# Mean rows of the context products in one operand of 36 partitions, and a last product that finishes its last two tiles one by one

## The chip, the cores and the metric

The kernel runs on one core of a Trainium2 chip, in one launch. The metric is the device time of an execution in microseconds. The core's engines run their own instruction streams and meet only at semaphores: PE (TensorE, matrix products into PSUM), DVE (VectorE), ACT (ScalarE), POOL (GpSimd) and SP, which here only issues transfers.

## The reference, cut to what matters

Three stages are added onto x (2 x 512 tokens, width 1024), in float32; each begins with a layer norm without weights:

```python
x = x + attn_block(layernorm(x))                 # Mamba2 block and a gated MLP of 3584
x = x + matmul(fake_quant(layernorm(x)), fake_quant(ctx))   # per batch [512,1024] x [1024,1024]
x = x + ffn(layernorm(x))                        # gate, up and down of 3584
# layernorm:  (x - mean) / sqrt(var + 1e-5)
# fake_quant: q = clip(round(x / s + zp), 0, 255);  (q - zp) * s
# ffn weights: W = base + mean(|w - base|) * sign(w - base)
```

Both inner widths are 3584, so that each of the two MLPs (m = 0 and m = 1 below) is three products of 1024 tokens with 1024 x 3584 weights.

## The kernel before, in words

**Layout.** x lies on the chip as x transposed: 128 channels on the partitions, 8 such tiles (`KT`) for 1024 tokens (`TOK`); a half of it is one batch of 512 tokens (`H`). One matmul has 128 x 128 weights and 512 columns. Products in float32 accuracy are made of three matmuls in a rounded format (hi x hi, lo x hi, hi x lo); ACT or DVE makes the hi parts, DVE the lo parts. The MLPs are computed by Winograd products of blocks: gate and up at L1067 (L1011 for a few plain ones ahead), down at L1092, as two blocks (`sc`) of 7 products (`t`) in each MLP, so that d = 14 m + 7 sc + t runs over 28 down products, and d = 27 is the last one of the program. A down product has 7 steps (k, `SC_PAIRS`), one per pair of weight tiles in a ring of 7 slots, and 4 output tiles (q) in 4 PSUM banks: 7 x 4 x 3 = 84 matmuls. `down_step` issues them step by step, with q inside k, so all four tiles end together; semaphore `s_pd` then tells DVE, which adds or subtracts the 4 tiles into x (`down_out`, L1914, one instruction of 128 x 512 each). In the last product of all, each such sum is followed by a store of the tile by SP (L739).

**Order.** PE executes in the order in which the code issues. First x's statistics (L848), then the Mamba2 block, MLP m = 0, the context stage, MLP m = 1. PE is not alone in setting the pace: in the context stage DVE and ACT normalise and round x while PE multiplies the rounded part of it. All weights of MLP m = 1 are made up by DVE, ACT and POOL ahead of PE, in the order of the steps (`ring_hi`, `ring_lo`, `comb_hi`, `comb_lo`).

**Context stage.** For each batch b, `ctx_first` (L1133 to L1144) walks the 8 input tiles k as ACT delivers them (`s_q1`) and makes 4 output tiles at once (L1125, integers in bf16); after each k a small matmul (L1139) multiplies row sums of the other operand, `g_parts`, 4 columns wide (three bf16 parts of the sum, and a column of ones), into rows 0 to 3 of a PSUM bank. ACT (`rows_hi`, L1643) and DVE (`rows_lo`, L2314) turn these rows, scaled by -1/1024, into a hi and a lo part of 4 rows each, two tiles of `xm_r`. `minus_mean` (L1130) then subtracts the mean over the output channels from an output tile with two matmuls of 3 rows, hi and lo, weights all one. The other 4 output tiles follow (`second_tile`). DVE takes each tile into x (`ctx_take`, L2327) and squares it; PE sums the squares for the variance (`ctx_var`, L1119, L1122). `second_mean` (L1148) makes the mean of the next layer norm from the 4 rows, hi and lo, as float32 matmuls, which are two instructions each. DVE takes that at L2320, then works out the next layer norm's scale and starts on the inputs of MLP m = 1, PE begins the products of m = 1 at L1011.

**Constants.** At the start DVE fills constants (L1690 ff.), scales for the quantisation (L1709 to L1716), and only then squares x (L2033), for which PE waits at L848.

## Time and profile before

| | |
|---|---|
| median of 3 runs | 2143.09 us (2141.26, 2143.09, 2144.04) |
| the profiled execution's own time | 2142.7 us |
| its span | 2140.9 us |
| mean granted TensorE clock over it | 0.993 of full |
| PE busy | 2101.9 us (98%), 9270 matmuls |
| DVE busy | 1664.3 us (78%) |
| ACT, POOL busy | 1071.0 us (50%), 182.5 us (9%) |
| PE in the chain that ended last | 87%; DVE 7%, ACT 3%, issue 2%, DMA 1% |

The span goes from the first to the last instruction that the profiler recorded, the execution's own time is 1.8 us longer. Busy time is time in which an instruction was in execution; that of PE counts matmuls, whose weight loads (PEld) overlap other matmuls. The chain that ended last follows the last instruction back to what it waited for, step by step; only a change to a piece in this chain can shorten the time at once, and then only until another chain takes its place.

### The profile page before, as it was taken

The numbers are of one execution on the slowest core, as the hardware profiler recorded it, in microseconds if no ns is written. First come the engines' busy times: TensorE is split into PE (matmuls) and PEld (weight loads), VectorE is DVE, ScalarE is ACT, GpSimd is POOL, SyncE is SP. The second block draws the span as 40 slices with busy tenths as digits, with TensorE's granted clock in tenths as the row PEclk, the third lists the DMA queues.
The fourth block names the chain that finished last, engine by engine and source line by source line (L and its number), as shares of the span: only waits on it lengthen the run. The fifth ranks groups of instructions, "written<-read, shape, count | busy, mean of one in ns | idle before, by whom it ended". The sixth has DMA issues, their size and how long they took to land.

```text
span 2140.9 us, 26618 instructions
## 1 busy us (share of the span) xinstructions
PE 2101.9 (98%) x9270; PEld 1680.6 (78%) x9270; DVE 1664.3 (78%) x2497; ACT 1071.0 (50%) x1764; POOL 182.5 (9%) x296
## 2 busy tenths in 40 slices
PE   7999999999999999999999999999999999999999
PEld 3777778777888888888888854888888888888887
DVE  7766666698777888887979888987777677698885
ACT  4333344466777777775444466543333333444442
POOL 0000110101111111210000001100010000100000
PEclk9999999999999999999999999999999999999999
DMA  3141115638989999889250043654444443856101
GB/s 123 40 169 66 59 60 171 160 78 293 316 285 316 344 323 340 307 313 341 83 193 1 1 151 101 174 197 151 177 151 145 175 148 135 301 186 202 56 20 59
DMA packets 136435, 370.06 MB, mean 173 GB/s; under 512 B 16689, under 2 KB 27569, under 8 KB 132657
## 3 DMA queue, kind: packets, MB, share of 16 engines
q1 hardware_dynamic: 111216, 288.16, 39.3%
q0 software_dynamic: 25088, 80.23, 11.0%
q8 instruction: 73, 1.20, 0.2%
q14 instruction: 58, 0.47, 0.1%
HBM read 288.12 MB, written 84.41 MB: 174 GB/s over the span
## 4 chain that ended last, share of the span: by engine, by line
PE 87%; DVE 7%; ACT 3%; issue 2%; DMA 1%; SPq 0%; DVEq 0%; ACTq 0%
PE pair L1067 42%; PE pair L1092 24%; PE pair L839 7%; PE pair L1011 4%; PE pair L832 2%; DVE conv_out L2098 1%; PE pair L1125 1%; PE pair L949 1%; PE pair L970 1%; DVE pair L1922 1%; DVE weights_lo L1688 1%; PE pair L848 1%; PE pair L1119 1%; PE pair L972 1%; PE pair L865 0%
## 5 line engine op out<-in xcount | busy, mean ns | idle before, releaser
L1067 PE MATMUL pair<-comb_hi,ring_hi 128*128 128x512 f32 x1456 | 567.0, 389 | 3.3 <-ACT gate_a L1400 3.3
L1067 PE MATMUL pair<-comb_hi,ring_lo 128*128 128x512 f32 x1456 | 566.5, 389 | 0.0
L1067 PE MATMUL pair<-comb_lo,ring_hi 128*128 128x512 f32 x1456 | 566.4, 389 | 0.0
L1092 PE MATMUL pair<-inner_ring_a,ring_hi 128*128 128x512 f32 x1120 | 344.9, 389 | 0.0
L1067 PEld LDWEIGHTS pair<-comb_hi,ring_hi 128*128 128x128 f32 x1456 | 273.3, 188 | 62.5 <-DVE ring_lo L1778 5.3
L1067 PEld LDWEIGHTS pair<-comb_lo,ring_hi 128*128 128x128 f32 x1456 | 273.4, 188 | 56.7
L1067 PEld LDWEIGHTS pair<-comb_hi,ring_lo 128*128 128x128 f32 x1456 | 273.3, 188 | 56.5
L1092 PEld LDWEIGHTS pair<-inner_ring_a,ring_hi 128*128 128x128 f32 x1120 | 210.2, 188 | 43.5
L1092 PE MATMUL pair<-inner_ring_a,ring_lo 128*128 128x512 f32 x560 | 217.9, 389 | 0.0
L1322 ACT ACTIVATE ring_hi<-ring_sum 128x512 fp32r<-128x512 f32 x160 | 101.4, 633 | 143.7 <-DVE ring_sum L1763 142.0
L1778 DVE TENSOR_TENSOR ring_lo<-raw_a,ring_hi 128x512 fp32r<-128x512 f32 x146 | 99.9, 689 | 52.6 <-ACT ring_hi L1322 52.6
L1092 PE MATMUL pair<-inner_ring_b,ring_hi 128*128 128x512 f32 x448 | 138.3, 390 | 0.0
L1448 ACT ACTIVATE sign_out<-pair 128x1024 int8<-128x1024 f32 x84 | 86.1, 1025 | 80.7 <-DVE pair L1922 80.7
L1092 PEld LDWEIGHTS pair<-inner_ring_a,ring_lo 128*128 128x128 f32 x560 | 105.1, 188 | 21.9
L1778 DVE TENSOR_TENSOR ring_lo<-ring_sum,ring_hi 128x512 fp32r<-128x512 f32 x160 | 110.0, 687 | 2.2 <-ACT ring_hi L1322 0.9
L839 PE MATMUL pair<-act_hi,weights_hi 128*128 128x512 f32 x256 | 109.4, 427 | 1.7 <-DVE act_lo L2167 1.4
L1922 DVE TENSOR_TENSOR pair<-coeff_in 128x1024 f32<-128x1024 f32 x84 | 103.2, 1228 | 0.0
L1688 DVE TENSOR_TENSOR weights_lo<-weights_raw,weights_hi 128x1024 fp32r<-128x1024 f32 x44 | 54.6, 1241 | 59.4 <-ACT weights_hi L1245 31.0
L839 PE MATMUL pair<-act_hi,weights_lo 128*128 128x512 f32 x256 | 100.3, 392 | 0.0
L839 PE MATMUL pair<-act_lo,weights_hi 128*128 128x512 f32 x256 | 100.1, 391 | 0.0
L1092 PEld LDWEIGHTS pair<-inner_ring_b,ring_hi 128*128 128x128 f32 x448 | 84.1, 188 | 17.8 <-issue 0.5
L1322 ACT ACTIVATE ring_hi<-raw_a 128x512 fp32r<-128x512 f32 x146 | 90.4, 626 | 10.7 <-DVE raw_a L1758 7.1
(374 smaller groups left out, 3591.8 us busy)
## 6 DMA issues: line engine op xcount, KB each, us to landing
coeff_in<-f_gu SPq DMA_DIRECT2D x56, 512.0 KB, 5.2
coeff_in<-b_gu SPq DMA_DIRECT2D x56, 512.0 KB, 6.8
weights_raw<-w_mamba SPq DMA_DIRECT2D x44, 512.0 KB, 3.5
raw_a<-w_gu SPq DMA_DIRECT2D x28, 512.0 KB, 7.1
raw_a<-w_gu SPq DMA_DIRECT2D x56, 256.0 KB, 6.3
u_spill<-gate_a POOLq DMA_DIRECT2D x56, 256.0 KB, 5.8
coeff_in<-f_dn SPq DMA_DIRECT2D x28, 512.0 KB, 4.3
coeff_in<-b_dn SPq DMA_DIRECT2D x28, 512.0 KB, 6.1
```

The source lines that it names most:

```text
L832: ins = pe.matmul(out[:, HALF[half]], w[:, wi, k * P:(k + 1) * P], a(half, k), start=k == 0 and n == 0, stop=k == KT - 1 and n == 2)
L839: ins = pe.matmul(out, w[:, wi, k * P:(k + 1) * P], a(b, k), start=k == 0 and n == 0, stop=k == KT - 1 and n == 2, skip_group_check=True)
L848: return pe.matmul(out[:, HALF[b]], ones[:, :], src[:, HALF[b]], start=first, stop=last)
L949: pe.matmul(ps[2][:, g * 512:(g + 1) * 512], bx_cur[:, 2 + g, :], xbc[:, 4 + g * HPG:4 + (g + 1) * HPG, b * SEQ + c * P:b * SEQ + (c + 1) ...
L1011: ins = pe.matmul(out, wt[:, slot, col], a, start=j % 2 == 0 and kk == 0 and n == 0, stop=j % 2 == 1 and kk == KH - 1 and n == 2, skip_gro ...
L1067: ins = pe.matmul(out, wt[:, slot, col], a, start=t in (0, 1, 3) and kk == 0 and n == 0, stop=kk == KH - 1 and n == 2, skip_group_check=True)
L1092: ins = pe.matmul(out, wt[:, slot, col], a, start=t in (0, 1, 3) and k == 0 and n == 0, stop=k == SC_PAIRS - 1 and n == 2, skip_group_chec ...
L1322: act.activation(WRH[:, slot, :], src, ACT.Copy).then_inc(s_whi, 1)
L1448: act.activation(sign_out[:, c % 2, :], dif_ps[:, :], ACT.Sign).then_inc(s_sign, 1)
L1688: TT(WL[:, slot, :], raw[:, rslot, :], WH[:, slot, :].bitcast(F32), ALU.subtract).then_inc(s_ready, 1)
L1778: TT(WRL[:, slot, :], src, WRH[:, slot, :].bitcast(F32), ALU.subtract).then_inc(s_wlo, 1)
L1922: TT(dif_ps[:, :], dif[:, c % 2, 0, :], dif[:, c % 2, 1, :], ALU.subtract).then_inc(s_cd, 1)
```

## The change

Two parts, and some small ones that they need.

**One operand for the mean rows.** `g_parts` is 36 columns wide: 0 to 2 and 32 to 34 hold the three parts, 3 and 35 are one, the others zero. The small matmul of `ctx_first` gives rows 0 to 35; `rows_hi` writes the rounded rows 0 to 35, `rows_lo` writes the rest over rows 32 to 35 of the same tile. So `minus_mean` and `second_mean` are one matmul of 36 rows in place of two of 3 or 4 rows. Their weights need a zero or a factor per row, which DVE works out at the start (four more small operations, a fifth one that was in `ctx_left_factors`, and two small memsets); `ctx_left_factors` becomes two instructions, `q2_parts` gets one more copy. The buffer `ones_rounded` moves, since `g_parts` grew, and is filled later, in `decay_rows`. The semaphore `s_dtc` is merged into `s_dts`.

**The last product.** `down_step` for d = 27 issues tiles q = 0 and 1 step by step (6 matmuls per step), then all 7 steps of q = 2 (21 matmuls), then all 7 of q = 3. `s_last` is raised after q = 1 and after q = 2, `s_pd` after q = 3, and `down_out` waits for them in turn.

The diff, cut:

```diff
@@ -274,11 +275,15 @@
-    def mean_rows(b, part):
-        return xm_r[0:4, 2 * part + b, 0:H]
-    ones_rows = xm_r[0:3, 4, 0:P]
-    row_weights = xm[0:4, 5, 0:P]
+    ROWS = slice(0, 36)
+    LOW_ROWS = slice(32, 36)
+    def mean_rows(b, rows):
+        return xm_r[rows, b, 0:H]
+    ones_rows = xm_r[ROWS, 4, 0:P]
+    row_weights = xm[ROWS, 5, 0:P]
...
@@ -372,11 +377,10 @@
     g_rest = small("q2_row_sums_rest", [P, CTX_TILES])
-    g_parts = small("q2_row_sums_bf16", [P, CTX_TILES, 4], BF16)
+    g_parts = small("q2_row_sums_bf16", [P, CTX_TILES, 36], BF16)
     mean_col = small("mean_columns", [P, 3, BATCH])
-    row_scale = small("row_scale", [P, 2])
+    row_scale = small("row_scale", [P, 4])
     pick = small("minus_head_pick", [P, HEADS])
-    ones_r = small("ones_rounded", [P, P], F32R)
     tri, ident, mask = shp[:, 0, :], shp[:, 1, :], shp[:, 2, :]
...
@@ -1068,6 +1072,21 @@
+        def last_tiles(w, m, k, qs):
+            slot, us = w % RING, (w - BASE_D[m]) % RING
+            for q in qs:
+                out = bank(4 + q)
+                col = slice(q * P, (q + 1) * P)
+                for n, (wt, a) in enumerate(((WRH, ur_hi(us)), (WRH, ur_lo(us)), (WRL, ur_hi(us)))):
+                    ins = pe.matmul(out, wt[:, slot, col], a, start=False,
+                                    stop=k == SC_PAIRS - 1 and n == 2, skip_group_check=True)
+                if k == SC_PAIRS - 1 and q == 1:
+                    ins.then_inc(s_last, 1)
+                elif k == SC_PAIRS - 1 and q == 2:
+                    ins.then_inc(s_last, 1)
+            if qs == (3,):
+                ins.then_inc(s_pd, 1)
         def down_step(w, m, sc, t, k):
...
@@ -1084,6 +1103,14 @@
                         pe.wait_ge(s_ab, CF_BLOCKS)
+            if m == 1 and d == 13:
+                last_tiles(w, m, k, (0, 1))
+                if k == SC_PAIRS - 1:
+                    for q in (2, 3):
+                        for kk in range(SC_PAIRS):
+                            last_tiles(w - k + kk, m, kk, (q,))
+                return
             slot, us = w % RING, u % RING
...
@@ -1126,9 +1153,7 @@
         def minus_mean(b, out):
-            for part in range(2):
-                ins = pe.matmul(out, ones_rows, mean_rows(b, part)[0:3], start=False, stop=part == 1, skip_group_check=True)
-            ins.then_inc(s_xo, 1)
+            pe.matmul(out, ones_rows, mean_rows(b, ROWS), start=False, stop=True, skip_group_check=True).then_inc(s_xo, 1)
...
@@ -1136,7 +1161,7 @@
                     ctx_mm(b, o, k, banks[o])
-                ins = pe.matmul(rows[0:4, :], g_parts[:, b * KT + k, :], q1[b][:, k, :], start=k == 0, stop=k == KT - 1)
+                ins = pe.matmul(rows[ROWS, :], g_parts[:, b * KT + k, :], q1[b][:, k, :], start=k == 0, stop=k == KT - 1)
                 if k == late:
...
@@ -1144,9 +1169,7 @@
         def second_mean(b, out):
-            for part in range(2):
-                ins = pe.matmul(out, row_weights, mean_rows(b, part).bitcast(F32), start=part == 0, stop=part == 1)
-            ins.then_inc(s_csumd, 1)
+            pe.matmul(out, row_weights, mean_rows(b, ROWS).bitcast(F32), start=True, stop=True).then_inc(s_csumd, 1)
...
@@ -1640,7 +1663,7 @@
             act.wait_ge(s_row, b + 1)
-            act.activation(mean_rows(b, 0), bank(5)[0:4, :], ACT.Copy, scale=-1.0 / DM).then_inc(s_rhi, 1)
+            act.activation(mean_rows(b, ROWS), bank(5)[ROWS, :], ACT.Copy, scale=-1.0 / DM).then_inc(s_rhi, 1)
...
@@ -1699,7 +1722,6 @@
         dve.memset(coef3[:, :], 0.0)
-        dve.tensor_copy(ones_r[:, :], ones[:, :])
         own.then(TT(pick[:, :], ident[:, 0:HEADS], ident[:, PART_AT[1]:PART_AT[1] + HEADS], ALU.add))
...
@@ -1714,6 +1736,14 @@
         own.then(TS(row_scale[:, 0:1], D2, -float(DM), 1.0, ALU.mult, ALU.add))
+        for first in (0, 32):
+            dve.memset(g_parts[:, :, first + 3:first + 4], 1.0)
+        own.then(TT(row_scale[:, 3:4], ident[:, 3:4], ident[:, 35:36], ALU.add))
+        own.then(TS(row_scale[:, 1:2], row_scale[:, 3:4], row_scale[:, 0:1], -1.0, ALU.mult, ALU.add))
+        own.then(dve.tensor_reduce(row_scale[:, 2:3], ident[:, 0:3], mybir.AxisListType.X, ALU.add))
+        own.then(dve.tensor_reduce(row_scale[:, 3:4], ident[:, 32:35], mybir.AxisListType.X, ALU.add))
+        own.then(TT(row_scale[:, 2:3], row_scale[:, 2:3], row_scale[:, 3:4], ALU.add))
...
@@ -1908,8 +1938,15 @@
                     dve.wait_ge(s_do, 4 * d)
-                dve.wait_ge(s_pd, w + 1)
+                if d < 27:
+                    dve.wait_ge(s_pd, w + 1)
                 for q in range(KH):
+                    if d == 27 and q == 0:
+                        dve.wait_ge(s_last, 1)
+                    elif d == 27 and q == 2:
+                        dve.wait_ge(s_last, 2)
+                    elif d == 27 and q == 3:
+                        dve.wait_ge(s_pd, w + 1)
                     tile = X[m][:, QROW[quad] + q, COL[m][QCOL[quad]]]
...
@@ -2000,11 +2037,13 @@
             hi, mid, lo = (g_parts[:, :, n] for n in range(3))
+            low_rows = g_parts[:, :, 32:35]
             own.then(dve.tensor_copy(hi, g_all[:, :]))
             own.then(TT(g_rest[:, :], g_all[:, :], hi, ALU.subtract))
             own.then(dve.tensor_copy(mid, g_rest[:, :]))
             own.then(TT(g_rest[:, :], g_rest[:, :], mid, ALU.subtract))
-            dve.tensor_copy(lo, g_rest[:, :]).then_inc(s_cp, 1)
+            own.then(dve.tensor_copy(lo, g_rest[:, :]))
+            dve.tensor_copy(low_rows, g_parts[:, :, 0:3]).then_inc(s_cp, 1)
...
@@ -2077,6 +2116,7 @@
             top = slice(0, PARTS_K)
+            dve.tensor_copy(ones_r[:, :], ones[:, :])
             own.then(dve.tensor_copy(cs_rows[top, :], ps[3][top, :]))
...
@@ -2276,9 +2316,8 @@
         def ctx_left_factors():
-            dve.tensor_copy(ones_rows, ones[0:3, :])
-            own.then(TS(row_scale[0:4, 1:2], shp[0:4, 1, 3:4], row_scale[0:4, 0:1], -1.0, ALU.mult, ALU.add))
-            TS(row_weights, ones[0:4, :], row_scale[0:4, 1:2], None, ALU.mult).then_inc(s_mc, 1)
+            TS(ones_rows, ones[ROWS, :], row_scale[ROWS, 2:3], None, ALU.mult)
+            TS(row_weights, ones[ROWS, :], row_scale[ROWS, 1:2], None, ALU.mult).then_inc(s_mc, 1)
...
@@ -2311,7 +2350,8 @@
             dve.wait_ge(s_rhi, b + 1)
-            STT(mean_rows(b, 1), bank(5)[0:4, :], -1.0 / DM, mean_rows(b, 0).bitcast(F32), ALU.mult, ALU.subtract).then_inc(s_rlo, 1)
+            STT(mean_rows(b, LOW_ROWS), bank(5)[LOW_ROWS, :], -1.0 / DM, mean_rows(b, LOW_ROWS).bitcast(F32),
+                ALU.mult, ALU.subtract).then_inc(s_rlo, 1)
...
```

On PE, at the end of the context stage, after the last tile of `second_tile` (`x_mid_rounded` is the tile with the mean rows). Before:

```order
L1130 MATMUL pair<-x_mid_rounded 128x512 x4
L1125 MATMUL pair<-q_1_162,q_163 128x512 x16
L1130 MATMUL pair<-x_mid_rounded 128x512 x4
L1119 MATMUL pair<-x_mid,ones_over_dm 128x512 x3
L1122 MATMUL pair<-x_mid,ones_over_dm 128x512 x2
L1148 MATMUL pair<-x_mid_rounded,x_mid 128x512 x4
L1011 MATMUL pair<-comb_hi_82,ring_hi 128x512
```

Now:

```order
L1156 MATMUL pair<-x_mid_rounded 128x512 x2
L1152 MATMUL pair<-q_1_163,q_164 128x512 x16
L1156 MATMUL pair<-x_mid_rounded 128x512 x2
L1146 MATMUL pair<-x_mid,ones_over_dm 128x512 x3
L1149 MATMUL pair<-x_mid,ones_over_dm 128x512 x2
L1172 MATMUL pair<-x_mid_rounded,x_mid 128x512 x2
L1015 MATMUL pair<-comb_hi_83,ring_hi 128x512
```

Every group of mean matmuls has half as many; what stands between them is in the same order. L1156 was L1130, L1172 was L1148, both with 36 rows now.

On PE, in the last product (`pair2` holds the banks of q = 0 and 1, `pair3` those of q = 2 and 3; x2 is two matmuls). Before, the last eight rows of the program:

```order
L1092 MATMUL pair2<-inner_ring_b_136,ring_hi_131 128x512 x2
L1092 MATMUL pair2<-inner_ring_b_136,ring_lo_132 128x512
L1092 MATMUL pair2<-inner_ring_b_136,ring_hi_131 128x512 x2
L1092 MATMUL pair2<-inner_ring_b_136,ring_lo_132 128x512
L1092 MATMUL pair3<-inner_ring_b_136,ring_hi_131 128x512 x2
L1092 MATMUL pair3<-inner_ring_b_136,ring_lo_132 128x512
L1092 MATMUL pair3<-inner_ring_b_136,ring_hi_131 128x512 x2
L1092 MATMUL pair3<-inner_ring_b_136,ring_lo_132 128x512
```

Now:

```order
L1081 MATMUL pair2<-inner_ring_b_137,ring_hi_132 128x512 x2
L1081 MATMUL pair2<-inner_ring_b_137,ring_lo_133 128x512
L1081 MATMUL pair2<-inner_ring_b_137,ring_hi_132 128x512 x2
L1081 MATMUL pair2<-inner_ring_b_137,ring_lo_133 128x512
L1081 MATMUL pair3<-inner_ring_a_135,ring_hi_132 128x512 x2
L1081 MATMUL pair3<-inner_ring_a_135,ring_lo_133 128x512
L1081 MATMUL pair3<-inner_ring_a_135,ring_hi_132 128x512 x2
L1081 MATMUL pair3<-inner_ring_a_135,ring_lo_133 128x512
```

Before, each step goes over both halves, and the four tiles end within 12 matmuls of each other. Now `pair2` ends first; behind it stand 42 matmuls, 21 on q = 2 and then 21 on q = 3, which begin again with the first inner tile (`inner_ring_a`).

On DVE, from the last constants to the first squares of x. Before:

```order
L1713 TENSOR_SCALAR quant_columns<-quant_columns 128x1
L1714 TENSOR_TENSOR quant_columns<-quant_columns 128x1
L1715 TENSOR_TENSOR quant_columns<-quant_columns 128x1
L1716 TENSOR_SCALAR row_scale<-quant_columns 128x1
L2033 TENSOR_TENSOR conv_out<-hs 128x512 x4
```

Now:

```order
L1736 TENSOR_TENSOR quant_columns<-quant_columns 128x1
L1737 TENSOR_TENSOR quant_columns<-quant_columns 128x1
L1738 TENSOR_SCALAR row_scale<-quant_columns 128x1
L1740 MEMSET q_row_sums_bf_190 128x16 x2
L1742 TENSOR_TENSOR row_scale<-tri_ident_mask 128x1
L1743 TENSOR_SCALAR row_scale<-row_scale 128x1
L1744 TENSOR_REDUCE row_scale<-tri_ident_mask 128x1
L1745 TENSOR_REDUCE row_scale<-tri_ident_mask 128x1
L1746 TENSOR_TENSOR row_scale<-row_scale 128x1
L2072 TENSOR_TENSOR conv_out<-hs 128x512 x4
```

Seven small instructions stand between L1738 (was L1716) and the squares L2072 (was L2033); five of them wait for one another through `own.then`. The cast of `ones_rounded`, 128 x 128, has gone from ahead of these rows.

## Rows read from the trace of the kernel before

**Rows 1.** The page: its first line and section 1.

```profile
span 2140.9 us, 26618 instructions
...
PE 2101.9 (98%) x9270; PEld 1680.6 (78%) x9270; DVE 1664.3 (78%) x2497; ACT 1071.0 (50%) x1764; POOL 182.5 (9%) x296
```

**Rows 2.** The chain that ended last, whole span: start us, us, what.

```profile
7.89 5.73 PE pair L848 x8
...
1373.74 495.27 PE pair L1067 x2184
```

**Rows 3.** The same chain, asked for from 1276 to 1332 us.

```profile
1297.20 0.31 PE pair L1139
1297.51 0.97 PE pair L1125 x4
...
1304.97 1.12 PE pair L1130 x4
...
1315.56 0.67 PE pair L1130 x2
...
1318.48 4.51 PE pair L1119 x6
...
1324.70 3.62 PE pair L1148 x8
```

**Rows 4.** Timeline of DVE: start us, us, engine line operation, [idle before <-releaser].

```profile
6.41 0.16 DVE L1715 TENSOR_TENSOR quant_columns<-quant_columns 128x1 f32<-128x1 f32 x1
6.60 0.15 DVE L1716 TENSOR_SCALAR row_scale<-quant_columns 128x1 f32<-128x1 f32 x1
7.05 0.69 DVE L2033 TENSOR_TENSOR conv_out<-hs 128x512 f32<-128x512 f32 x1 [0.29 <-DMA hs<-x_t]
8.76 0.69 DVE L2033 TENSOR_TENSOR conv_out<-hs 128x512 f32<-128x512 f32 x1 [1.02 <-DMA hs<-x_t]
```

**Rows 5.** Groups by form: line engine operation, shapes xcount | busy us, mean ns | idle before.

```profile
L917 PEld LDWEIGHTS pair<-tri_ident_mask,minus_cs_wide 128*72 128x72 f32 x16 | 1.8, 143 | 0.1
...
L1139 PEld LDWEIGHTS pair<-q,q_row_sums_bf 128*4 128x4 bf16 x16 | 1.3, 80 | 6.8 <-issue 6.8
```

**Rows 6.** The same view for PE.

```profile
L942 PE MATMUL pair<-cs_rhs,ones_rounded 72*128 72x512 f32 x16 | 5.2, 404 | 2.9 <-DVE conv_out L2098 2.9
```

**Rows 7.** Timeline of DVE around the context stage.

```profile
1280.30 0.69 DVE L2292 SCALAR_TENSOR_TENSOR scratch_c<-scratch_c 128x512 f32<-128x512 f32 x1 [1.47 <-ACT scratch_c L1619]
...
1316.33 1.41 DVE L2327 SCALAR_TENSOR_TENSOR centred<-pair,quant_columns,centred 128x512 f32<-128x512 f32 x2 [2.08 <-PE pair L1130]
...
1328.44 0.75 DVE L2320 SCALAR_TENSOR_TENSOR scratch_c<-pair,quant_columns,scratch_c 128x512 f32<-128x512 f32 x1 [0.97 <-PE pair L1148]
...
1369.93 0.70 DVE L1778 TENSOR_TENSOR ring_lo<-raw_even,ring_hi 128x512 fp32r<-128x512 f32 x1
```

**Rows 8.** Timeline of PE at the wait for ACT, and at product step 15.

```profile
1296.16 1.04 PE L1125 MATMUL pair<-q,q 128*128 128x512 bf16 x4 [0.44 <-ACT q L1628]
...
1370.84 0.40 PE L1011 MATMUL pair<-comb_hi,ring_hi 128*128 128x512 f32 x1
```

**Rows 9.** Stretches: start:end, length, PE busy (instructions), granted clock, DMA share, GB/s.

```profile
980.00:1240.00 260.00, 260.00 (x1147) 1.00 0.29 102
1318.40:1324.60 6.20, 6.12 (x10) 0.72 0.15 56
```

**Rows 10.** The same for DVE: length, DVE busy.

```profile
1328.50:1370.60 42.10, 41.60 (x66) 0.96 0.84 193
```

**Rows 11.** Timeline of DVE and SP at the end.

```profile
2121.47 0.69 DVE L1809 TENSOR_TENSOR inner_ring_b<-inner_ring_b_f,inner_ring_b 128x512 fp32r<-128x512 f32 x1
2135.70 2.48 DVE L1914 TENSOR_TENSOR x_last<-x_last,pair 128x512 f32<-128x512 f32 x4 [13.54 <-PE pair L1092]
...
2138.21 0.33 SPq L739 DMA_DIRECT2D out_t<-x_last  x1
```

**Rows 12.** The stores of the output, line L739.

```profile
DMA to landing us min/median/max: 2.0/2.2/2.3
```

More of the change, by code:

```diff
@@ L220, in build @@
     cs_rows = at("cs_rows", H0 + 27 * KB, [P, TOK], F32R)
+    ones_r = at("ones_rounded", H0 + 31 * KB, [P, P], F32R)
     R0 = 96 * KB
@@ L422, in build @@
     s_dtm, s_dte, s_dts, s_csx = (sem(n) for n in ("dt_and_cs_summed", "dt_exp_in", "dt_and_cs_act", "cs_exp_in"))
-    s_dtc = sem("dt_rows_copied")
     s_hpair = sem("head_pairs_summed")
@@ L459, in build @@
     s_xq = [sem(f"x_quarter_in{i}") for i in range(4)]
+    s_last = sem("last_tiles_done")
     s_do, s_x2, s_out = sem("down_taken"), sem("x2_stored"), sem("out_stored")
@@ L899, in _ @@
         conv_pair(1)
-        pe.wait_ge(s_dtc, 1)
+        pe.wait_ge(s_dts, 1)
         pe.wait_ge(s_ht, BATCH + 1)
@@ L1515, in _ @@
         act.wait_ge(s_dtm, 1)
-        act.activation(dt_rows, ps[2][0:2 * HEADS, :], ACT.Copy).then_inc(s_dtc, 1)
+        act.activation(dt_rows, ps[2][0:2 * HEADS, :], ACT.Copy).then_inc(s_dts, 1)
         root(1, scr_u)
@@ L1692, in _ @@
         dve.memset(ones_mean[:, :], 1.0 / DM)
-        dve.memset(g_parts[:, :, :], 1.0)
+        dve.memset(g_parts[:, :, :], 0.0)
         dve.sem_inc(s_conv, 2)
@@ L2121, in _ @@
         TS(ncs_all[:, :, :], ncs_all[:, :, :], -1.0, None, ALU.mult).then_inc(s_dte, 1)
-        dve.wait_ge(s_dts, 1)
+        dve.wait_ge(s_dts, 2)
         TS(a_all[:, :, :], ncs_all[:, :, :], 1.0, None, ALU.add).then_inc(s_dte, 1)
@@ L2131, in _ @@
         own.then(TT(ncs_all[:, :, :], ncs_all[:, :, :], dend_all[:, :, :], ALU.mult))
-        dve.wait_ge(s_dts, 3)
+        dve.wait_ge(s_dts, 4)
         own.then(TT(ncs_all[:, :, :], ncs_all[:, :, :], gtot_all[:, :, :], ALU.mult))
@@ L2155, in _ @@
         conv_pair(CONV_TILES // 2 - 1, decay_rows)
-        dve.wait_ge(s_dts, 5)
+        dve.wait_ge(s_dts, 6)
         dve.wait_ge(s_silu, CONV_TILES)
```

## The prediction

> **What bounds the kernel now.** I read the page first: PE is busy in 2101.9 of 2140.9 us [rows 1]. Then the chain of waits over the whole span, to see where PE's work is the chain: one piece of 495.27 us with 2184 matmuls has no wait in it, and it gives the unit, 495.27 / 2184 = 0.227 us for one 128 x 512 matmul [rows 2]. A matmul taken away is worth that where PE is the chain. Then the chain around the context stage, piece by piece [rows 3], and the timelines of the engines that PE waits for, at the start [rows 4], in the context stage [rows 7, 8] and at the end [rows 11]. The chain says which wait ends last; the timelines say how much later than its cover it ends, and that is what an edit can win there.
>
> The sum is made against the profiled execution, 2142.7 us, which is 0.4 under the median of 2143.09.
>
> **The start: +0.5.** DVE's small constants follow each other every 0.19 us (6.41 to 6.60), and the last ends at 6.75; the squares of x begin at 7.05, released by a transfer, 0.29 after DVE came free [rows 4]. Seven small instructions now stand between. Five depend on one another: 5 x 0.19 = 0.95, the two memsets issue between, and the cast of 128 x 128 that is gone took about as little as one of these (I take 0.1 to 0.2). So DVE comes to its first square about 0.8 later and 0.8 - 0.29 = 0.5 of it shows. PE's 5.73 us of L848 hangs on that square without a gap [rows 2]; the second pair waits for its transfer until 8.76 whatever happens [rows 4], so a part could be absorbed. Ends: 0 (the later transfers decide) and +0.8. I take +0.5, nearer to the row that is tied to the first square.
>
> **The small matmul with 36 columns: +0.4.** L1139 stands every fifth matmul in the chain. It takes 0.31, a neighbour in its group of four 0.97 / 4 = 0.24 [rows 3]. A weight load of 4 columns takes 80 ns, one of 72 takes 143 [rows 5]; between them 36 columns are about 80 + 32/68 x 63 = 110 ns, 0.03 more. Twelve of the 16 lie where PE does not wait for ACT: 12 x 0.03 = 0.4. Ends: 0, if the load stays beside the matmul before it, and 12 x 0.06 = 0.75, if it costs as the load of 72.
> The row shows that the small matmul is 0.07 longer than its neighbours, though its 4-column load is the shortest of all. The Trainium skill (page "TensorE: Matmul & The Clock Gate", section "Step-by-step: what each phase is for") has it that the next weights are pulled ahead of the running matmul, so that a load hides behind it; by that this term would be 0 and the sum 0.4 lower. The trace does not quite agree here, with 0.31 against 0.24; the sum goes by the rows.
>
> **The mean rows on PE in the middle: -1.6.** A group of four mean matmuls takes 1.12 us [rows 3]; there are eight groups, and two of four matmuls go in each, 2 x 0.227 = 0.45 each. Which of them counts is set by the one wait between: PE waits 0.44 at 1296.16 for ACT's q [rows 8]. What ACT does there goes back to DVE's chain that starts at 1280.30, released by ACT [rows 7], not by PE's mean matmuls. So the four groups of the first batch only lengthen that wait, and are worth nothing. Behind it are three whole groups up to the take at 1316.33, 3 x 0.45 = 1.35, and in the last one DVE waits for the first tile alone, one matmul of two: 0.24 more, 1.6 in all. DVE waits 2.08 us there [rows 7], so it is ready for the earlier time. Ends: 0.9, if only two groups pass on, and 1.8.
>
> Behind that, PE sums the squares. In 1318.40 to 1324.60 ten matmuls take 6.20 us at a granted clock of 0.72, where in 980 to 1240 it is 1.00 [rows 9]: the clock is at its lower level, 1.2 GHz, for a part of it, after PE had waited for DVE's squares. Everything there moves together, PE's wait stays (DVE takes and squares with the same durations), and I take the fall as it is. Rival B is about that.
>
> **The second mean: -1.75.** Eight float32 instructions of L1148 take 3.62 us [rows 3], 0.45 each; four go: -1.8. DVE waits for this matmul at 1328.44 (0.97 of idle) and from there it is busy for 41.60 of 42.10 us [rows 7, 10], up to the lo part at 1369.93, which ends at 1370.63; PE begins the step that uses it at 1370.84 [rows 7, 8]. So PE has 0.2 in hand over DVE; PE and DVE both move up by nearly the whole amount, since both hang on L1148. I take 1.75. Ends: 0, if something else holds DVE, and 1.8.
>
> **Constants and copies inside: 0.** The cast in `decay_rows` and the copy in `q2_parts` are one DVE instruction each. For the second the cover is PE's own work: PE is busy for 260.00 of 260.00 us in 980 to 1240 [rows 9]. Without cover they cost about 0.2 each.
>
> **The tail: -1.9.** DVE's four adds run 2.48 us behind the end of PE, and the last store is issued at 2138.21 [rows 11]. With tiles 0 to 2 done under PE's last 21 matmuls (21 x 0.227 = 4.8 us for an add of 0.68), only one add stays: 2.48 - 0.68 = -1.8. The store itself takes 2.0 to 2.3 us from issue to landing [rows 12]; the last one has the queue to itself now and may be at the lower end, -0.1. All 84 matmuls stay. The new order brings steps nearer together: q = 0 and 1 need an operand pair every 6 x 0.227 = 1.36 us instead of 2.7. PE's product ends at 2135.6, so it starts at 2135.6 - 84 x 0.227 = 2116.5, and needs the seventh pair at 2116.5 + 6 x 1.36 = 2124.7; DVE's last split ends at 2122.16 [rows 11]. So 2.5 us are in hand. Ends: -1.5 and -2.1.
>
> **Sum.** +0.5 + 0.4 - 1.6 - 1.75 - 1.9 = -4.35. 2142.7 - 4.35 = 2138.35, and I say 2138.4.
>
> **The rivals.**
> *B, the clock does not fall.* PE arrives sooner at its wait ahead of L1119. If the lower level is not granted there, its ten float32 matmuls in 6.20 us [rows 9] take as long as those of L1148, 0.45 each [rows 3]: 4.5, 1.7 less. DVE still has to make the squares for them, which may hold back a part; I take 1.3: 2137.1. For it: PE does less ahead of this wait, and no row here ties the fall to a place. Against it: the wait before it is unchanged.
> *C, the middle is absorbed.* Two groups instead of three pass on (+0.7), the start costs +0.8 (+0.3), the 36 columns +0.75 (+0.35), and the second mean gives 0.4 less because DVE's 0.2 in hand turns into a wait: about 1.8 more, 2140.1. For it: three engines hand over to each other within a few tenths [rows 7, 8, 10]. Against it: the chain there shows PE on both sides of every hand-over.
> *D, the last product stalls* on its inner tiles, and the 1.9 of the tail are lost: 2140.3. Against it: 2.5 us in hand.
> *E, slower.* A matmul with 36 rows takes f times the one of 3 or 4 rows. Seven mean matmuls stay on the chain between 1296.16 and 1316.33, and four instructions of the second mean: 7 x 0.227 + 4 x 0.45 = 3.4 us, each extra unit of f adds that. The rest of the sum stays, so 2138.4 + 3.4 (f - 1): level at f = 2.3, and at f = 2.5 2143.5. Against it: a matmul of 72 rows takes 404 ns [rows 6], one of 128 rows 400 [rows 8], with nothing that grows with rows.
>
> **How the numbers follow.** The forecast holds with a chance of 0.47, B 0.17, C 0.22, D 0.08, E 0.06. About 0.2% (4.3 us) is what a measurement of this kernel can tell from no change, so against the median faster begins under 2138.8. The forecast lies just on the faster side of that: I give it 0.33 of its 0.47 there and 0.14 inside, B wholly faster, C 0.19 within and 0.03 faster, D within, E 0.03 within and 0.03 slower (over 2147.4, from f = 3.6). That makes 0.53 faster, 0.44 the same, 0.03 slower. The range goes from 2136.0 (B, and the low ends of the tail and start) to 2141.2 (C and D with the runs' own spread of 2.8 us).
>
> **What would show it.** In the profile of the changed kernel: the first L848 0.5 later; 0.34 for the small matmul; a longer wait of PE for ACT's q, near 2.2 in place of 0.44; the mean groups at half of 1.12; four instructions for the second mean in 1.8; the first step of MLP m = 1 3.3 - 0.9 = some 2.4 earlier; between PE's last matmul and the last store one add. Wrong it would be if PE's wait for q stays at 0.44 (then all eight groups count), if the last product shows a gap, or if the clock in 1318 to 1325 comes out at 1.00.

## The result, and the profile after

| | before | changed |
|---|---|---|
| median | 2143.14 us (8 runs, 2139.32 to 2145.38) | 2137.51 us (8 runs, 2136.21 to 2138.72) |
| the profiled execution's own time, its span | 2142.7, 2140.9 us | 2136.38, 2134.6 us |

The ratio is 0.9976, with a 95% interval of 0.9965 to 0.9986: 5.1 us less, between 3.0 and 7.5. The forecast of 2138.4 was 0.9 too high. The two profiles differ by 6.3 us, more than the medians (5.6), because the profiled execution of the changed kernel is 1.1 us under its own median and that of the kernel before 0.4. The 6.3 can be laid out in full.

The page of the changed kernel:

```profile
span 2134.6 us, 26585 instructions
...
PE 2093.8 (98%) x9250; PEld 1675.7 (79%) x9250; DVE 1665.2 (78%) x2504; ACT 1069.3 (50%) x1764; POOL 181.9 (9%) x296
```

The chain that ended last (start us, us, what), at the start, in the context stage and at the long run of the second MLP, which answers to [rows 2, 3]. Line numbers have moved: L848 is L852, L1139 is L1164, L1130 is L1156, L1125 is L1152, L1119 is L1146, L1148 is L1172, L1067 is L1071, and the last product is L1081. L852 is the sum of squares at the start, L1152 the integer products, L1164 the small matmul, L1156 the mean, L1071 the long run.

```profile
8.21 5.48 PE pair L852 x8
...
15.85 7.15 PE pair L852 x16
...
1296.20 1.04 PE pair L1152 x4
1297.24 0.32 PE pair L1164
1297.56 0.97 PE pair L1152 x4
...
1305.06 0.66 PE pair L1156 x2
...
1314.27 0.44 PE pair L1156
...
1369.58 495.29 PE pair L1071 x2184
...
2112.39 19.05 PE pair L1081 x84
```

The timeline of PE at its waits in that stretch (start us, us, what, idle before and its releaser), which answers to [rows 8] (L1146 sums the squares):

```profile
1292.71 0.82 PE L1152 MATMUL pair<-q,q 128*128 128x512 bf16 x3 [1.12 <-ACT q L1651]
1296.20 1.04 PE L1152 MATMUL pair<-q,q 128*128 128x512 bf16 x4 [0.41 <-ACT q L1651]
1316.95 2.81 PE L1146 MATMUL pair<-x_mid,ones_over_dm 128*128 128x512 f32 x6 [2.02 <-DVE x_mid L2325]
```

The first of these sums of squares took 4.51 us for the same six instructions before [rows 3]. The stretches (length, PE busy, granted clock) say why; 1316.90 to 1323.20 answers to the second of [rows 9]:

```profile
1316.90:1323.20 6.30, 6.25 (x14) 1.00 0.14 54
1323.20:1329.80 6.60, 6.58 (x28) 1.00 0.64 82
```

PE has 14 instructions in 6.3 us where it had 10, at a granted clock of 1.00 in place of 0.72. A fall is from here on a stretch of some 3 us in which the granted clock is at its lower level, near 0.5 of full. Before, there was a second fall behind the first, in the first products of the second MLP. The two stretches of the kernel before show it, and the next row is PE's wait in the changed kernel, late in the same products:

```profile
1324.60:1328.20 3.60, 3.60 (x9) 1.00 0.00 0
1329.50:1333.00 3.50, 3.50 (x10) 0.51 1.00 120
```

```profile
1366.57 0.50 PE L1015 MATMUL pair<-comb_hi,ring_hi 128*128 128x512 f32 x1 [0.98 <-DVE ring_lo L1808]
```

Neither fall is left, and PE is now so early that it waits for DVE, for 0.98 us here and for 0.16 and 0.24 in two places near 1330.

DVE's timeline, first around the context stage, then at the end, with SP's last store (compare [rows 7] and [rows 11]):

```profile
1314.80 1.41 DVE L2367 SCALAR_TENSOR_TENSOR centred<-pair,quant_columns,centred 128x512 f32<-128x512 f32 x2 [0.90 <-PE pair L1156]
```

```profile
2117.33 0.68 DVE L1839 TENSOR_TENSOR inner_ring_b<-inner_ring_b_f,inner_ring_b 128x512 fp32r<-128x512 f32 x1
2122.05 1.28 DVE L1951 TENSOR_TENSOR x_last<-x_last,pair 128x512 f32<-128x512 f32 x2 [4.03 <-PE pair L1081]
2126.71 0.69 DVE L1951 TENSOR_TENSOR x_last<-x_last,pair 128x512 f32<-128x512 f32 x1 [3.38 <-PE pair L1081]
2131.47 0.69 DVE L1951 TENSOR_TENSOR x_last<-x_last,pair 128x512 f32<-128x512 f32 x1 [4.07 <-PE pair L1081]
```

```profile
2132.18 0.33 SPq L743 DMA_DIRECT2D out_t<-x_last  x1
```

Laid out at five landmarks, in us of each profile ("q" is the moment at which PE resumes behind ACT's q, "the run" the start of the long run):

| from | to | before | changed | difference |
|---|---|---|---|---|
| start | q | 1296.16 | 1296.20 | 0.0 |
| q | DVE's last take (L2327, L2367) | 20.17 | 18.60 | -1.6 |
| DVE's last take | the run of 2184 matmuls | 57.41 | 54.78 | -2.6 |
| the run | PE's end (2135.58, 2131.44) | 761.8 | 761.9 | 0.0 |
| PE's end | end of the span | 5.3 | 3.2 | -2.2 |

The 0.0 of the first row holds for these two executions only: in the other profiles below PE resumes between 1294.75 and 1299.40. The row in the middle is the one that needed the experiments: 2.6, where 1.75 was forecast. The intervals behind the landmarks are the differences of starts in the rows: 1373.74 - 1316.33 = 57.41 before [rows 2, 7], 1369.58 - 1314.80 = 54.78 now.

### The profile page after: what moved, and what is told of

It is laid out like the page before. It is cut to its first block, busy times and chain, and to the rows that moved or that the text cites. A ratio compares the mean times of both kernels' runs of the same rounds, so it can differ in the third digit from the quotient of the medians.

```text
span 2134.6 us, 26585 instructions
## 1 busy us (share of the span) xinstructions
PE 2093.8 (98%) x9250; PEld 1675.7 (79%) x9250; DVE 1665.2 (78%) x2504; ACT 1069.3 (50%) x1764; POOL 181.9 (9%) x296
## 4 chain that ended last, share of the span: by engine, by line
PE 83%; DVE 10%; ACT 4%; issue 2%; DMA 1%; SPq 0%; DVEq 0%; ACTq 0%
PE pair L1071 41%; PE pair L1119 24%; PE pair L843 7%; PE pair L1015 2%; PE pair L836 2%; DVE conv_out L2138 1%; DVE pair L1959 1%; PE pair L1081 1%; PE pair L1152 1%; PE pair L953 1%; PE pair L974 1%; DVE weights_lo L1711 1%; PE pair L852 1%; DMA sign_in_ab<-sign_spill 1%; DVE ring_lo L1808 1%
## 5 line engine op out<-in xcount | busy, mean ns | idle before, releaser
L1071 PE MATMUL pair<-comb_hi,ring_hi 128*128 128x512 f32 x1456 | 567.7, 390 | 3.4 <-ACT gate_a L1423 3.4
L1071 PE MATMUL pair<-comb_hi,ring_lo 128*128 128x512 f32 x1456 | 567.1, 389 | 0.0
L1071 PE MATMUL pair<-comb_lo,ring_hi 128*128 128x512 f32 x1456 | 567.0, 389 | 0.0
L1119 PE MATMUL pair<-inner_ring_a,ring_hi 128*128 128x512 f32 x1080 | 332.8, 390 | 0.0
L1071 PEld LDWEIGHTS pair<-comb_hi,ring_hi 128*128 128x128 f32 x1456 | 273.4, 188 | 62.4 <-DVE ring_lo L1808 5.4
L1071 PEld LDWEIGHTS pair<-comb_hi,ring_lo 128*128 128x128 f32 x1456 | 273.4, 188 | 56.9
L1071 PEld LDWEIGHTS pair<-comb_lo,ring_hi 128*128 128x128 f32 x1456 | 273.5, 188 | 56.2
L1119 PEld LDWEIGHTS pair<-inner_ring_a,ring_hi 128*128 128x128 f32 x1080 | 202.7, 188 | 42.0
L1119 PE MATMUL pair<-inner_ring_a,ring_lo 128*128 128x512 f32 x540 | 210.3, 389 | 0.0
L1119 PE MATMUL pair<-inner_ring_b,ring_hi 128*128 128x512 f32 x432 | 133.5, 390 | 0.0
L1119 PEld LDWEIGHTS pair<-inner_ring_a,ring_lo 128*128 128x128 f32 x540 | 101.4, 188 | 21.0
L1711 DVE TENSOR_TENSOR weights_lo<-weights_raw,weights_hi 128x1024 fp32r<-128x1024 f32 x44 | 54.7, 1244 | 59.4 <-ACT weights_hi L1268 31.1
L1119 PEld LDWEIGHTS pair<-inner_ring_b,ring_hi 128*128 128x128 f32 x432 | 81.1, 188 | 17.2 <-issue 0.5
```

What stands on the lines that cost most here:

```text
L1071: ins = pe.matmul(out, wt[:, slot, col], a, start=t in (0, 1, 3) and kk == 0 and n == 0, stop=kk == KH - 1 and n == 2, skip_group_check=True)
L1119: ins = pe.matmul(out, wt[:, slot, col], a, start=t in (0, 1, 3) and k == 0 and n == 0, stop=k == SC_PAIRS - 1 and n == 2, skip_group_chec ...
L1711: TT(WL[:, slot, :], raw[:, rslot, :], WH[:, slot, :].bitcast(F32), ALU.subtract).then_inc(s_ready, 1)
```

## The experiments

All ran 8 to 11 times, those of a group beside 28 to 33 runs of the kernel before on the same chip. Single profiles carry the details; the ratios carry the verdicts.

**The two parts apart.** The kernel before with the last product of the changed one (and the merged semaphore):

```diff
+            if m == 1 and d == 13:
+                last_tiles(w, m, k, (0, 1))
...
```

> Only the last product is changed, with the mean rows as before. Theory A (the tail saves what its own rows show, whatever the middle does): PE's last product starts at the same time as before, one add of 0.69 us is left behind it instead of 2.48, and the span is 2.0 to 2.2 us shorter, near 2141.0 against 2143.1. The clock falls near 1319 and 1330 stay as in the kernel before. Theory B (the whole 5.6 us come from a fall of the clock that the changed program happens to miss, the tail is covered anyway): under 0.5 us shorter.

Measured: 2140.50 us, ratio 0.9994 (0.9985 to 1.0003). The span of its profile is 2138.6, 2.3 less than before, and its DVE has one add behind PE's end, at 2135.44. Both falls are in its profile. Theory A holds in the profile; the ratio alone (1.3 us less, from 3.2 less to 0.6 more) does not tell it from nothing.

The mean rows in 36 partitions, with the last product of before:

```diff
-            if m == 1 and d == 13:
+            if False:
...
```

> Only the mean rows in 36 partitions, with the last product as before. Theory A (the parts add up: the changed kernel's first step of the second MLP's long run comes 4.2 us earlier in the profile, 1.5 by the mean matmuls, 1.7 by the second mean, the rest by the clock): 3.3 to 4.2 us under the kernel before, some 2139.3, with a granted clock of 1.00 in the sums of squares. Theory B (the middle's gain is only the 2.4 us forecast, the rest of the profile's difference is the one execution that was profiled): 2.4 us, 2140.7, with the fall of the clock back in the profile.

Measured: 2138.46 us, ratio 0.9982 (0.9973 to 0.9991), 3.9 us less, and no fall at this place in its profile. That is theory A. The two parts, 1.3 and 3.9, add up to the 5.1 of both, each with an interval of some 2 us to either side.

**Where the middle's gain comes from.** The second means twice, the mean matmuls once:

```diff
+            pe.matmul(out, row_weights, mean_rows(b, ROWS).bitcast(F32), start=True, stop=True)
             pe.matmul(out, row_weights, mean_rows(b, ROWS).bitcast(F32), start=True, stop=True).then_inc(s_csumd, 1)
```

> The changed kernel with each second mean computed twice over the same rows, so that PE has the eight float32 instructions of before again. Theory A (PE's path goes through the second mean): the first step of the second MLP starts 1.8 us later. DVE takes the second mean at 1324.5 + about 1.1, since it was itself busy until 1323.1, and from there all is DVE's: 1.0 to 1.3 us over the changed kernel, near 2138.7. Theory B (the second mean's time is hidden beside DVE's own work): 0 to 0.3 us, 2137.6. Theory C (a longer stretch of float32 matmuls brings the clock's fall back): 2.5 us or more, with a granted clock under 0.8 near 1325 to 1330.

Measured: 2137.51 us, ratio 0.9978 (0.9969 to 0.9987), as the changed kernel's. By its profile the long run starts at 1369.17 and DVE's last take at 1313.48: 55.7 between them, 0.9 more than in the changed kernel. So the profile speaks for theory A, the median for B, and 0.9 is about what medians of some ten such runs can't tell. C is out: the clock is 1.00 from 1278 to 2130.

Filling PE's wait in the kernel before:

```diff
+        for k in range(KT):
+            pe.matmul(bank(5), q2[:, KT + k, 0:P], q1[1][:, k, :], start=True, stop=True, skip_group_check=True)
         pe.wait_ge(s_ht, 4 + BATCH + 2)
```

> The kernel before, with eight more bf16 matmuls (of no use, into a bank that is free) in PE's 1.8 us wait ahead of the last sums of squares, so that PE is not idle there. Theory A (the fall of the clock at 1319 follows on PE's idle time): no fall in 1318 to 1325 and none at 1330, the sums of squares take 4.5 instead of 6.2, and the time is 1.5 to 3 us shorter, 2140 to 2141.5, though PE does more. Theory B (the fall comes from something else, as transfers or chance of the execution): the fall stands at the same place, and the time is the same or 0.1 longer, 2143.2.

Measured: 2143.45 us, ratio 1.0001 (0.9992 to 1.0010). In the profile the first fall is gone (the six instructions of L1119 take 2.81), but another comes near 1325 to 1328:

```profile
1323.00:1328.00 5.00, 5.00 (x12) 0.69 0.38 54
```

In that profile the stretch from DVE's last take (1314.90) to the long run (1370.77) is 55.9 us in place of 57.4, so it did gain 1.5 there. But the profiled execution, at 2139.72, is the second fastest of eleven that go up to 2146.04, and the median is that of the kernel before. Neither theory is met: one execution without the first fall is shown, and whether the others have it no run tells.

**Rows or number?** By then the likeliest reason seemed to be that the few rows do it: matmuls of 3 and 4 rows bring the clock down, those of 36 do not. Two kernels part this. The first has 36 rows, the number of before and the new last product:

```diff
+            pe.matmul(out, ones_rows, mean_rows(b, ROWS), start=False, stop=False, skip_group_check=True)
             pe.matmul(out, ones_rows, mean_rows(b, ROWS), start=False, stop=True, skip_group_check=True).then_inc(s_xo, 1)
...
+            pe.matmul(out, row_weights, mean_rows(b, ROWS).bitcast(F32), start=True, stop=True)
```

> The changed kernel with every mean matmul and both second means issued twice, so that PE has as many of them as before, but all with 36 rows (the first batch's and the second's mean is thus subtracted twice: the result leaves the reference). Theory R (matmuls of 3 and 4 rows bring the clock down, those of 36 do not): no fall in 1316 to 1333, a spread of the runs near 1 us as in the changed kernel, and only PE's added work shows: 1.6 us for the mean matmuls and 0 to 0.3 for the second means over the changed kernel, 2139.3, which is 3.6 under the kernel before. Theory N (what counts is the number of the matmuls): falls as before, a spread of 2 us, and 2141.0.

The second is the kernel before with 3 and 4 rows and the number of the changed kernel, in `minus_mean` and in `second_mean`:

```diff
-            for part in range(2):
+            for part in range(1):
...
```

> The kernel before with the hi part of the mean rows alone: one matmul of 3 rows and one of 4 rows instead of two each (the low part is left out of the means). The last product is as before. PE has as few matmuls as in the run with the 36 rows alone, which had 2138.5. Theory R (few rows bring the clock down): a fall is left in 1316 to 1333 in the profile, the spread of the runs is nearer to 2 us than to 1, and the time 1 to 2 us over 2138.5, at 2139.5 to 2140.5. Theory N (the number counts): 2138.1 to 2138.5 (it has no added work at the start), a spread near 1 us, no fall.

Measured: both twice 2141.32 us, ratio 0.9993 (0.9984 to 1.0002); one part 2138.55 us, ratio 0.9979 (0.9969 to 0.9988). The stretches of the sums of squares and of what follows, of both twice:

```profile
1318.90:1325.20 6.30, 6.15 (x10) 0.73 0.16 59
1328.80:1333.20 4.40, 4.40 (x13) 0.61 0.79 108
```

and of one part:

```profile
1317.90:1324.20 6.30, 6.24 (x14) 1.00 0.14 54
1324.30:1333.20 8.90, 8.48 (x35) 1.00 0.77 104
```

By time and by profile theory R has fallen in both. With 36 rows and the old number the falls stand where they stood; with 3 and 4 rows and half the number they are gone. The spread of the runs, by which both expectations also went, speaks for neither theory: 3.1 us in eleven runs of both twice, 6.1 in ten of one part. Both twice has only the last product's gain left, one part has the gain of the 36 rows without having 36 rows. What the operand of 36 partitions buys is the halved number, nothing else.

**Which of the mean matmuls.** The first batch's twice, and the second batch's twice:

```diff
+            if b == 0:
+                pe.matmul(out, ones_rows, mean_rows(b, ROWS), start=False, stop=False, skip_group_check=True)
```

> The changed kernel with the mean matmuls of the first batch issued twice (the first batch's mean is subtracted twice), those of the second once. Theory A (as forecast: the first batch's mean matmuls only shorten PE's wait for ACT's q): PE's wait at 1292.7 goes, the last wait at 1296.2 stays near 0.4, the last take of DVE stays at 1314.8, the time is 2137.5. Theory B (the clock's fall follows on how long PE has been busy without a pause): the pause of 1.1 us at 1291.6 is gone, and the falls near 1319 and 1330 are back: 1.7 to 2.7 us more, 2139.2 to 2140.2.

> The changed kernel with the mean matmuls of the second batch issued twice (its mean is subtracted twice), those of the first once. Theory A (as forecast): the last take of DVE comes 1.5 to 1.6 us later, at 1316.3, and all behind it too: 2139.0 if the clock stays at 1.00. Theory B (the pause of 1.1 us in the first batch is what spares the clock): no fall, 2139.0. Theory C (what counts is where the sums of squares lie in time, 1317 against 1318.5): falls as before, 2141.0.

and all of them twice, the second mean once (the first line above without its condition, as in the run with both twice):

> The changed kernel with all mean matmuls issued twice (both means are subtracted twice), the second mean once. It has the falls of the run with both twice if the mean matmuls set them: then PE sets the pace behind DVE's last take and the halved second mean is worth its 1.7 us: 1.7 less than the run with both twice, 2139.6. If there is no fall: last take 1.6 later, 2139.1.

Measured: first batch twice 2137.75 us, ratio 0.9981 (0.9972 to 0.9990), its last wait for q 0.38, no fall, long run 54.8 behind the last take: theory A, and B is out: PE's pause of 1.1 us is gone and the clock stays. Second batch twice 2140.82 us, ratio 0.9990 (0.9981 to 0.9999), with the first fall: nearest to C. All twice 2139.08 us, ratio 0.9988 (0.9979 to 0.9997), with the first fall. Neither has the second. PE's sums of squares in the profile of the first batch twice, and then of the second batch twice:

```profile
1317.22 2.81 PE L1146 MATMUL pair<-x_mid,ones_over_dm 128*128 128x512 f32 x6 [2.02 <-DVE x_mid L2327]
```

```profile
1321.78 4.51 PE L1146 MATMUL pair<-x_mid,ones_over_dm 128*128 128x512 f32 x6 [1.79 <-DVE x_mid L2327]
```

The same two numbers part all profiles: 4.51 behind a wait of 1.8 in the five kernels with four mean matmuls per group in the second batch (before, last product alone, both twice, second batch twice, all twice), and 2.81 in all those with two and in the one whose wait was filled. Five against nine is no accident, though each kernel has one profile. But for the filled wait, the first fall goes with the number, and with half of it PE comes to the sums of squares 20.8 us after it took up q in place of 22.3 (1316.95 - 1296.20, and 1318.48 - 1296.16).

With these profiles the stretch from DVE's last take to the long run can be read as a table, in us:

| | eight instructions of second mean | four |
|---|---|---|
| clock falls in the sums of squares | 57.4 (before; both twice 57.4) | 55.7 (second batch twice; all twice 55.7) |
| clock stays there | 55.7 (second twice) | 54.8 (changed; one part 54.6) |

The second fall, near 1330, is in the upper left corner alone, and it costs nothing there. Two stretches of the kernel before and of all twice:

```profile
1328.00:1333.00 5.00, 5.00 (x15) 0.66 0.75 87
```

```profile
1328.00:1333.00 5.00, 5.00 (x23) 1.00 0.64 73
```

From DVE's take of the last second mean it is 45.30 us to the long run in the kernel before (1373.74 - 1328.44) and 45.27 in all twice (1373.52 - 1328.25): DVE sets the pace there, and PE's fall runs beside it. So down the left column the first fall costs 1.7, which is what its six instructions lose (4.51 - 2.81), and across the upper row the second mean costs 1.7, as forecast for a kernel in which the fall stays. Together they give 2.6 and not 3.4. In the last corner PE is ahead and DVE sets the pace up to its take of the second mean: 8.97 us from the last take (1323.77 - 1314.80), where all twice has 10.40 (1328.25 - 1317.85), and without the fall's 1.70 would have 8.70. Behind it DVE waits once for a transfer, at 1355.6, for which it does not wait in the kernel before. The row is from the changed kernel's waits (us, times, longest):

```profile
DVE raw_odd L1983 <- DMA sign_in_ab<-sign_spill: 0.5, 1, 0.5
```

**The start.** The five small operations moved into `q2_parts`:

```diff
             dve.wait_ge(s_g, CTX_TILES)
+            own.then(TT(row_scale[:, 3:4], ident[:, 3:4], ident[:, 35:36], ALU.add))
...
```

> The changed kernel with the five small operations on the row factors moved from ahead of the first squares to the place where the row sums are split, where DVE has time. Theory A (the delay of the start is swallowed by later waits for transfers): the first square starts 0.3 us earlier, the end of the first third is where it was, and the time is the changed kernel's within 0.3: 2137.4. Theory B (the start passes its delay on to the end, as forecast): 0.5 shorter, 2137.0.

Measured: 2137.74 us, ratio 0.9974 (0.9964 to 0.9984): nothing, theory A. In its profile the first square waits for the transfer again (0.52 of idle) and begins at 7.16, against 7.37, and PE's next group of L852 begins at 16.36, against 15.85. That execution has a fall near 16 us which the changed kernel's does not have, so its profile says little on the later steps; the time does.

**Two ways further.** The second means ahead of the sums of squares:

```diff
+        pe.wait_ge(s_xt, KT + 6)
+        second_mean(0, bank(6))
+        second_mean(1, bank(3))
         pe.wait_ge(s_ht, 4 + BATCH + 2)
         ctx_var(bank(7), x_square, range(3), KT + 3 * KH, (6, 7), 5 * KT)
-        second_mean(0, bank(6))
-        second_mean(1, bank(3))
```

> The changed kernel with both second means issued ahead of the last sums of squares, in PE's wait of 2.0 us for DVE's squares. Theory A (DVE sets the pace from 1314 to 1366 in the changed kernel): PE reaches the second MLP 1.8 us earlier and waits that much more for DVE's lo parts; DVE takes the second mean without the 0.5 and 0.3 us of waiting that it has at 1322.6 and 1323.5, so 0.6 to 0.8 shorter, 2136.8. Theory B (PE sets the pace): 1.8 shorter, 2135.7. Theory C (the banks that the second means need come free too late): no gain.

Measured: 2137.86 us, ratio 0.9975 (0.9965 to 0.9984), no gain. (One of its ten runs took 11199.7 us; nothing explains it.) By the profile the long run comes 54.7 after the last take, 0.1 less than in the changed kernel. The two short waits of DVE that I had read off the chain, 0.5 and 0.3, are pieces called issue there, and no idle time: DVE's timeline of the changed kernel has one instruction behind the other at that place,

```profile
1321.72 1.47 DVE L1880 TENSOR_TENSOR comb_lo<-comb_hi_f,comb_hi 128x512 fp32r<-128x512 f32 x2
1323.11 1.41 DVE L2360 SCALAR_TENSOR_TENSOR scratch_c<-pair,quant_columns,scratch_c 128x512 f32<-128x512 f32 x2
```

so that nothing was to be had from an earlier second mean. The number is theory C's, the reason is not: the banks came free in time, and PE's wait of 2.02 ahead of the sums of squares shrank to 0.31. PE, which comes earlier in this experiment, waits that much longer for its next operand:

```profile
1331.04 0.47 PE L1015 MATMUL pair<-comb_hi,ring_hi 128*128 128x512 f32 x1 [1.88 <-DVE comb_lo L1881]
```

And the last but one tile's mean before the last tile's products, which lets DVE take it while it idles:

```diff
         second_tile(1, 6, 1)
+        minus_mean(1, bank(1))
         pe.wait_ge(s_xt, KT + 2)
         second_tile(1, 7, 2)
-        minus_mean(1, bank(1))
         minus_mean(1, bank(2))
```

> The changed kernel with the mean matmul of the last but one output tile issued before the last tile's eight products instead of behind them. Theory A (from DVE's last takes to 1366 DVE sets the pace): DVE takes that tile in its 0.9 us of idle time ahead of 1314.8 and the last one at 1315.0, so it is through with both at 1315.7 instead of 1316.2, and the long run of the second MLP starts 0.5 us earlier: 2137.0. Theory B (PE sets it): PE's own order has no less in it, 2137.5.

Measured: 2136.62 us, ratio 0.9973 (0.9964 to 0.9982). The take moves into the idle time, and the squares follow the last one at 1315.58:

```profile
1313.40 0.74 DVE L2367 SCALAR_TENSOR_TENSOR centred<-pair,quant_columns,centred 128x512 f32<-128x512 f32 x1
1314.91 0.75 DVE L2367 SCALAR_TENSOR_TENSOR centred<-pair,quant_columns,centred 128x512 f32<-128x512 f32 x1 [0.76 <-PE pair L1156]
1315.58 1.88 DVE L2325 TENSOR_TENSOR x_mid<-x_mid 128x512 f32<-128x512 f32 x3
```

From PE's resumption behind q to the long run it takes 1368.48 - 1295.78 = 72.7 us, where the changed kernel takes 1369.58 - 1296.20 = 73.4. That looks like theory A's 0.5, but it is not: up to DVE's take of the second mean only 0.1 is won (1322.56 - 1295.78 = 26.78 against 1323.11 - 1296.20 = 26.91), since the last tile's take still waits for PE, for 0.76 where it was 0.90. The rest is the wait of 0.49 for `sign_in_ab`, which this execution does not have. It is the fastest kernel here by median; by ratio it can't be told from the changed one.

## Why the prediction was right

The time fell inside the range and near the forecast, and the terms that make up most of it, the mean rows and the tail, hold with their mechanism. Not all of it was insight. In the profiles the gain is 6.3 where 4.35 was forecast. Two of the prediction's three signs of being wrong came true: the last wait for q stayed, at 0.41, and the clock in 1318 to 1325 was 1.00. The first turned out harmless, the second is rival B.

**The start, +0.5 forecast: wrong, 0.** The first square came 0.32 later (7.37 against 7.05). The seven instructions took 1.1 us, more than the 0.95 worked out, but the constants ahead of them ended 0.5 sooner (6.24 against 6.75), because the transfer for which DVE waits first had landed sooner and a cast was gone. Of the 0.32 little went on: PE's first eight matmuls took 5.48 in place of 5.73, and the next group began 0.07 later. The later pairs arrive with their transfers. The low end of the range was the right one, and the term should have gone to it, since the second pair's wait of 1.02 [rows 4] was larger than the whole delay.

**The 36 columns, +0.4 forecast: 0.1.** The load takes 94 ns (80 before, 110 expected), and the small matmul 0.32 in place of 0.31 in the chain: 12 x 0.01. The rule of the Trainium skill (page "TensorE: Matmul & The Clock Gate", section "Step-by-step: what each phase is for") that the next load hides behind the running matmul, by which this term is 0, came nearer than the interpolation. The 0.08 that the small matmul takes beyond its neighbours is still there.

**The mean rows, -1.6 forecast: -1.6.** Groups of two take 0.66 against 1.12, which is 0.46 less and not the half that the prediction named as a sign; three groups and a first matmul count, those of the first batch do not. The run with the first batch twice shows that part by itself. The wait did not grow at its last place, as I had expected (2.2 us at 1296); it came up earlier in the same walk, 1.12 at 1292.71 and 0.5 before it.

**The second mean, -1.75 forecast, and the clock, 0 forecast: -2.6 together.** The step that failed is "I take the fall as it is". Rival B is what happened, and its 1.3 was too much because DVE and a transfer bound it: the table above gives 0.9 for it on top of the second mean. It comes from the first fall alone. I had put the reason on PE's unchanged wait. The wait is about the same (1.8, 2.0), and the clock falls behind the one and not the other.

**The tail, -1.9 forecast: -2.2.** One add is left, 0.69. The rest is 0.1 in the handing over from PE to DVE (2131.44 to 2131.47, where it was 0.13) and 0.3 at the last store: from its issue to the end of the span 2.4 us (2134.6 - 2132.18), where it was 2.7 (2140.9 - 2138.21). I had given that 0.1. No operand was late; the fear of rival D is met by the splits' end at 2118.0, 2.6 before the need at 2112.4 + 6 x 1.36 = 2120.6.

**The sum.** -4.35 was forecast and -6.3 came in the profiles: 0.8 at the start and the columns, 0.9 in the clock, 0.3 in the tail, all to the same side. The medians of 8 runs each differ by 5.6, which is 1.3 more than forecast, and the ratio says 5.1; that the forecast was only 0.9 too high is luck to the extent of 0.4, since it was set against an execution of 2142.7 and not against the median. E did not happen: 36 rows cost what 3 rows cost, 0.66 for a group of two either way (0.67 in the chain for two of 3 rows [rows 3]).

What stays open is why the clock falls with the old number and not with the new. The runs show that the first fall goes with the number of mean matmuls in the second batch, not with their rows. It does not go with the length of PE's wait: there is no fall behind 1.60 us (PE's wait at 1316.40 in the last experiment), a fall behind 1.8 and none behind 2.0. Whether it is the 1.5 us by which PE comes earlier, or the work it did before, no run tells apart.

## What to carry to other kernels

A matmul of 3 or 4 rows cost as much here as one of 36 (0.66 us for two), so operands of a few rows belong stacked on the partitions of one. Look for places where the granted clock falls before you price an edit of their neighbourhood: here eight fewer mean matmuls in the second batch went with two falls fewer, of which the first was worth 0.9 of the 6.3 us and the second nothing, as DVE set the pace beside it. A fall costs time only where its engine sets the pace. And where a store ends the program, let the tiles end one after the other: the adds of all but the last are free under the matmuls.

## What the runs showed of the hardware that I had not expected

The first fall of the clock is tied to the program's timing: 4.51 us or 2.81 us for the same six instructions, to the hundredth, in five and nine profiles. Other falls change from execution to execution. The changed kernel and the one with the second mean twice have the same code up to the context stage, and in 144 to 152 us the granted clock is 0.79 in the one profile and 1.00 in the other, in 1256 to 1264 again 0.79 and 1.00; the profile of the second batch twice alone has a fall near 794. So a single profile can have a fall more or less which no edit explains. My estimate is up to 1.7 us for each, from the first fall's 4.51 - 2.81.

The times of executions carry it too. In the 33 runs of the kernel before that stand beside the first four experiments, those with a mean granted clock of 0.995 average 2139.9 us (5 runs), those with 0.992 average 2144.3 (9 runs). The 8 runs of the changed kernel have only 0.994 and 0.995, but its spread of 2.5 us is no mark of a missing fall: the kernel with the first batch twice, without a fall at this place in its profile, spreads over 6.7 us in eleven runs.
